# Six expert tiles run between the steps of the last batch's routing, in one block

## The reference

```python
x = x + jnp.tanh(g_xattn[0]) * _L0_xattn_ref(_layernorm(x, axis=-1), ctx_1024, L0_xattn_Wq, L0_xattn_Wkv, L0_xattn_Wc)
x = x + jnp.tanh(g_ffn[0]) * _L0_ffn_ref(_layernorm(x, axis=-1), L0_ffn_gate_w, L0_ffn_w1, ...)
# in _L0_ffn_ref:
logits = jnp.einsum('btd,de->bte', x, gate_w)
top_v, top_i = jax.lax.top_k(logits, TOP_K)
top_w = jax.nn.softmax(top_v, axis=-1)
comb = jnp.zeros((N, E), dtype=x.dtype).at[jnp.arange(N)[:, None], idx].add(wts)
for e in range(E):
    h = jax.nn.gelu(xf @ w1[e] + b1[e], approximate=False)
    out = out + comb[:, e:e + 1] * (h @ w2[e] + b2[e])
```

## Time and profile before

| what | value |
|---|---|
| device time, median of 3 runs | 993.09 us (992.86 to 994.03) |
| span of the profiled execution | 992.7 us |
| PE busy | 832.3 us, 84% of the span |
| DVE, POOL, ACT busy | 517.9, 438.1, 376.7 us |
| share of PE in the chain that ended last | 43%; issue 1%, DMA 1%, all else under 1% |

### The profile page before, as it was taken

One profiled execution on the slowest core, in us unless ns is written; L12 is line 12 of the kernel. 1 busy time (PEld: TensorE's weight loads), 2 busy tenths in 40 slices (PEclk: granted clock), 3 DMA queues, 4 the chain that ended last, 5 costly groups with the idle time before them and its releaser, 6 DMA issues. The chain is left out here.

```text
span 992.7 us, 20863 instructions
## 1 busy us (share of the span) xinstructions
PE 832.3 (84%) x6508; PEld 579.8 (58%) x6509; DVE 517.9 (52%) x1534; ACT 376.7 (38%) x770; POOL 438.1 (44%) x475
## 2 busy tenths in 40 slices
PE   3675899899898989887610899999999999999994
PEld 1243345344343534433310699899989989988984
DVE  3475567766766677762330345444544454454451
ACT  1312263636363544666320333333333433333330
POOL 4766463666566545436541033333433343333334
PEclk9867899989997989898755799999999999999998
DMA  4653424433445261244224122221332233223210
GB/s 160 147 108 107 75 66 90 129 82 108 97 128 98 64 136 49 82 134 138 77 74 165 56 44 46 48 45 33 56 48 41 43 58 48 43 47 49 44 14 1
DMA packets 65691, 76.40 MB, mean 77 GB/s; under 512 B 7392, under 2 KB 59360, under 8 KB 65504
## 3 DMA queue, kind: packets, MB, share of 16 engines
q1 hardware_dynamic: 51328, 58.74, 22.7%
q0 software_dynamic: 14304, 16.93, 9.6%
HBM read 47.68 MB, written 29.53 MB: 78 GB/s over the span
## 5 line engine op out<-in xcount | busy, mean ns | idle before, releaser
L2389 PE MATMUL ps_h<-x_hi,w_split 128*128 128x256 bf16 x1248 | 212.7, 274 | 0.0
L2403 PE MATMUL ps_y<-w_split,hidden 128*128 x1248 | 206.4, 273 | 0.0
L698 ACT ACTIVATE prob<-ps_a 128x512 f32<-128x512 f32 x192 | 113.0, 603 | 181.5 <-PE ps_a L1127 108.2
L2389 PE MATMUL ps_h<-x_lo,w_split 128*128 128x256 bf16 x624 | 171.0, 274 | 0.0
L2403 PE MATMUL ps_y<-w_split,h_lo 128*128 x624 | 170.1, 273 | 0.0
L2299 ACT ACTIVATE hidden<-ps_h,bias 128x256 f32<-128x256 f32 x312 | 131.1, 471 | 88.6 <-PE ps_h L2389 88.6
L849 DVE TENSOR_REDUCE row_max<-ps_d 128x2 f32<-128x384 f32 x237 | 127.9, 551 | 60.8 <-PE ps_d L1107 59.2
L2273 POOL DMA_INDIRECT out<-y,token_at x78 | 131.0, 1680 | 43.8 <-POOL token_at L2271 30.3
L2389 PEld LDWEIGHTS ps_h<-x_hi,w_split 128*128 x1248 | 122.8, 98 | 14.5
L2403 PEld LDWEIGHTS ps_y<-w_split,hidden 128*128 128x128 bf16 x1248 | 122.1, 98 | 14.1
L2269 POOL TENSOR_TENSOR token_f<-tails,ones_f 128x2 f32<-128x2 f32 x39 | 7.8, 200 | 267.5 <-DVE y L2345 266.3
(11 more groups left out here) (206 smaller groups left out, 1070.8 us busy)
## 6 DMA issues: line engine op xcount, KB each, us to landing
w_stage<-w SPq DMA_DIRECT2D x32, 512.0 KB, 4.1
xg<-queue SPq DMA_DIRECT2D x39, 260.0 KB, 2.8
w_split<-q_split SPq DMA_DIRECT2D x24, 256.0 KB, 7.9
x_in<-x SPq DMA_DIRECT2D x8, 512.0 KB, 3.8
ctx_sb<-ctx_t SPq DMA_DIRECT2D x8, 512.0 KB, 3.6
x<-x SPq DMA_DIRECT2D x8, 512.0 KB, 3.8
q_split<-q_hl SPq DMA_DIRECT2D x16, 256.0 KB, 3.5
out<-x SPq DMA_DIRECT2D x8, 512.0 KB, 5.0
```

Of the source, the lines that this page charges most:

```text
L698: a.activation(prob[n % 2][:, j, :], ps_a[i % 2][:], ACT.Exp, scale=SCALE).then_inc(exp_ready, 1)
L2389: last = t_.matmul(ps_h[n][:, c, :], k.w1_split[:, bass.ds(e, 1), part, kt, f].rearrange("p a f -> p (a f)"), xs[s][:, kt, :], start=(q == ...
L2403: last = t_.matmul(ps_y[s][:, t, :], hs[s][:, f, token], k.w2_split[:, bass.ds(e, 1), part, f, :].rearrange("p a d -> p (a d)"), start=(q ...
```

## The change

The passes stop after p = 7. The last batch's routing now shares a new stretch with the first six tiles (`EARLY`). These are full tiles of 256 rows, taken from what the first six batches have put into the queues; `early_tables` on DVE works them out in pass 7, at step 2. The stretch is a list of 44 parts, `tile_parts()`: quarters of `layer1` and `layer2` (12 matmuls each), and the routing steps, now numbered by part (`END_*`), stand between them. `layer2` of tile 5 is left to the loop. The queues' remaining rows make 33 more tiles (`late_tables`). There is one block: no end of block stands between the two halves, and `in_general` comes between the stretch of 44 parts and the loop. PSUM is shared: `ps_x` is the bank `ps_r`, `ps_h` the banks `ps_d` and `ps_a`, and `ps_y` is the one bank `ps_o`, where before there were two. In the parts each quarter reads the expert number for itself. The last four pieces of the weights, the scatters of batches 6 and 7 and the adds of tiles 0 to 4 fall into the same stretch.

```diff
+EARLY = 6
+EARLY_BATCHES = 6
+PAIRS = FC // 2
...
+def early_tables(v, chain, k, scratch, ready, count):
+
+    chain.then(v.tensor_scalar(k.pad_f[:], k.n_queued[:], -float(TILE - 1), None, ALU.add))
+    tile_tables(v, chain, k, scratch, 0, EARLY, k.pad_f, k.queue_at)
+    chain.step(v.tensor_scalar(k.tiles_end[:], k.tiles_end[:], float(EARLY), None, ALU.min))
+    chain.then(v.tensor_scalar(k.tiles_start[:], k.tiles_start[:], float(EARLY), None, ALU.min))
+    chain.then(v.tensor_tensor(k.taken[:], k.tiles_end[:], k.tiles_start[:], ALU.subtract))
+    chain.then(v.tensor_scalar(k.taken[:], k.taken[:], float(TILE), None, ALU.mult))
+    v.tensor_tensor(k.rest_at[:], k.queue_at[:], k.taken[:], ALU.add).then_inc(ready, 1)
+    chain.engine.wait_ge(ready, count)
...
+        SP_EARLY, DVE_EARLY, PE_EARLY, ACT_EARLY = 18, 2, 29, 31
+        END_PIECES = (0, 12, 15, 18)
+        END_WEIGHTED, END_SUMS, END_TURN_SUMS, END_TAKE_HEADS = 1, 2, 3, 4
+        END_TURN_HEADS, END_COPY_HEADS, END_OUT, END_ADD, END_STATS = 5, 6, (7, 8), (8, 9), (9, 9, 10, 10)
+        END_MOMENTS, END_DEVIATION, END_SHIFT, END_ROWS = 10, 11, 12, 13
+        END_TURN_ROWS, END_COPY_ROWS, END_GATE, END_COPY_GATE, END_TURN_GATE = 15, 16, 17, 18, 19
+        END_CHOOSE, END_RATIO, END_RANK, END_SHARES, END_QUEUE = 20, 21, 22, 22, 23
...
+        def tile_parts():
+
+            parts = []
+            for i in range(EARLY):
+                parts += [(1, i, n) for n in range(PAIRS)]
+                if i:
+                    parts += [(2, i - 1, n) for n in range(PAIRS)]
+            return parts
...
         def each_step():
-            for p in range(-4, B + 2):
+            for p in range(-4, B):
...
+            chain.restart()
+            for step, (layer, i, n) in enumerate(tile_parts()):
+                if step == 0:
+                    queue_slots(LAST - 1)
+                    k.prepare(dve, chain, 0)
+                if step == END_TAKE_HEADS:
+                    take_heads(LAST, QUAD - 1)
...
+                if step == END_QUEUE:
+                    queue_slots(LAST)
+                    pad_places(v, chain, k, pads_placed)
+                    dve.wait_ge(pads_placed, 1)
+                    late_tables(v, chain, k, heads[:].rearrange("p t d -> p (t d)"), k.tables_ready, 3)
+                if layer == 1:
+                    if n == 0 and i + 1 < EARLY:
+                        k.prepare(dve, chain, i + 1)
+                    k.low(dve, i, n)
+                elif n == PAIRS - 1:
+                    k.finish(dve, i)
...
+            for step, (layer, i, n) in enumerate(tile_parts()):
+                if step == END_WEIGHTED:
+                    weighted(LAST, UNITS - 1)
+                if step == END_TURN_SUMS:
+                    turn_sums(LAST, QUAD - 1)
...
+                if layer == 1:
+                    if n == 0 and i + 1 < EARLY:
+                        turn_tile(i + 1)
...
+                    k.layer1(pe, i, n)
+                else:
+                    if (i, n) == (0, 0):
+                        bank_o.wait_read(pe)
+                    k.layer2(pe, i, n)
+            pe.wait_ge(w_lo, N_PIECES)
...
+        def layer1(pe, i, n, at=None, e=None):
+            s, _ = slot_of(i, at)
+            e = load_expert(pe, i) if e is None else e
...
+            turn(pe, EARLY)
+            all_layer2(pe, EARLY - 1)
             over_tiles(pe, body)
-            layer2(N_TILES - 1, (N_TILES - 1) % 2)
+            all_layer2(pe, N_TILES - 1)
```

More of the change, by code:

```diff
@@ L18 @@
 FAR = 1e30
+Q_AT = (5, 7, 6)
 SLOT_TILES = 2
@@ new lines, in split_x, with gelu @@
+        def split_x(act, i, at=None):
+            s, _ = slot_of(i, at)
+            act.wait_ge(x_turned, i + 1)
+            nc.scalar.copy(x_hi[s][:], ps_x).then_inc(x_hi_ready, 1)
+        def gelu(act, i, n, at=None):
+            s, _ = slot_of(i, at)
+            if n == 0 and not first(i, 2):
+                act.wait_ge(y_summed, i - 1)
+            act.wait_ge(h_ready, PAIRS * i + n + 1)
+            for c in range(2):
+                f = 2 * n + c
+                last = nc.scalar.activation(hidden[s][:, f, :], ps_h[n][:, c, :], ACT.Gelu, bias=bias[s][:, f:f + 1])
+            last.then_inc(gelu_done, 1)
@@ new lines, in experts, with all_layer1, all_layer2 @@
+        k.load, k.load_bias, k.add, k.split_x, k.gelu = load, load_bias, add, split_x, gelu
+        k.prepare, k.low, k.finish, k.turn, k.layer1, k.layer2 = prepare, low, finish, turn, layer1, layer2
+        def all_layer1(pe, i, at=None):
+            e = load_expert(pe, i)
+            for n in range(PAIRS):
+                layer1(pe, i, n, at, e)
+        def all_layer2(pe, i, at=None):
+            e = load_expert(pe, i)
+            for n in range(PAIRS):
+                layer2(pe, i, n, at, e)
@@ L2302, in _ @@
-            split_x(0, 0)
+                    gelu(act, i, n, (s, half))
+            split_x(act, EARLY)
             over_tiles(act, body)
@@ new lines, in early @@
+                late_tables(v, chain, k, scratch, k.tables_ready, 5)
+                for i in range(EARLY):
+                    prepare(dve, chain, i)
+                    for n in range(PAIRS):
+                        low(dve, i, n)
+                    if i:
+                        finish(dve, i - 1, early=added_again)
+                after_add(dve, EARLY - 2, added_again)
+                chain.restart()
+            pipeline.dve(dve)
+            in_general(dve, general[0].dve, general[1].dve, nothing, early)
@@ L2408, in body @@
+            pipeline.pe(pe)
+            in_general(pe, general[0].pe, general[1].pe, nothing, early)
             def body(i, half, s, more, two_more):
                 if more:
-                    turn(i + 1, half + s, 1 - s)
-                layer1(i, s)
-                if not first(i):
-                    layer2(i - 1, 1 - s)
-            turn(0, 0, 0)
+                    turn(pe, i + 1, (1 - s, half + s))
+                all_layer1(pe, i, (s, half))
+                if after_early(i):
+                    all_layer2(pe, i - 1, (1 - s, None))
```

607 lines of the change are left out of this document (391 added, 216 removed).

## The result

The changed kernel takes 964.51 us (median of 4 runs, 963.72 to 966.45); before it was 992.98 (4 runs, 991.54 to 994.03). The ratio is 0.9714, with a 95% interval of 0.9694 to 0.9734. The profiled execution has a span of 964.3 us. One execution among the experiments, of branch_else, took 1233.77 us at a mean granted clock of 0.647, where the kernel's other six had 0.938 to 0.945; the ratios leave it out.

The account below looks back on a forecast made before the run. PE bounds the loop at 10.92 us a tile but idles in the routing stretch before it. Loop start 581.6, plus 365.6 for tiles, 2.0 low clock and 13.1 end, gave span 962.3, median 963; own range 957 to 969, wider 946 to 977.

Parts of the forecast that it names:

- lateness by the early tables: Pass 7: `early_tables` ahead of `take_heads` on DVE delays batch 6's routing; 2.3 us remain, bounds 0 and 3.8.
- waits on the routing: In the 44 parts PE waits for routing pieces from other engines: 6.4 us, of which 2.4 at the turn of tile 2.
- register reads: In the 44 parts each quarter's read of the expert number outlasts PE's lead: 13 us, bounds 0 and 19.
- low clock: At the start of the stretch PE, nearly idle before, runs at half speed: 2.3 us.
- gap at the branch: `in_general` between quarter 44 and the loop leaves PE idle for 4.2 us, bounds 2.5 and 4.55.
- low clock behind it: A second low-clock spell after PE's idle gap at the branch: 2.0 us, bounds 0 and 4.
- rival of hidden loads: In the stretch PE's sequencer runs ahead, so some 3 of the 13 us of loads remain: 951 us, chance 0.25.
- rival of more waits: PE's waits let the clock fall inside the stretch, and lateness grows to 3.8: 970 to 980 us, chance 0.13.
- rival of half clock in all of the stretch: The stretch stays at half clock, about 141 us in place of 90.7: 1013 us, chance 0.03.
- One bank for `ps_y`: Rival: layer2 waits for the previous tile's `finish`; 4.2 us of loop room, else up to 1011 us; chance 0.05.
- The hidden chain: Scatter, pads and load of first loop rows end about 83 us into the stretch, ahead of PE at 95.
- 0.4 between span and median: Last step of the sum: the median stands 0.4 us above the profiled span, so 962.3 gives 963.

Follow-up runs that it names:

- branch_else: The changed kernel with the loop written on both sides of the branch, so the branch is not taken with these inputs: 959.35 us, ratio to before 0.9671.
- one_load: The changed kernel with PE reading the expert number once for four quarters, 11 reads in place of 44: 951.21 us, ratio to before 0.9588.
- no_general: The changed kernel without the read of `wide`, its branch and the general program: 959.63 us, ratio to before 0.9664.
- three_else: The changed kernel with one register read per four quarters, weight piece at part 6, `take_heads` one part earlier, loop on both branch sides: 943.56 us, ratio 0.9518.
- early4: The changed kernel with four early tiles in place of six (`EARLY = 4`): 973.52 us, ratio to before 0.9803.

## Why the prediction was right

The forecast was 963 with a range of 946 to 977; 964.51 lies in it. The steps, against the profiled execution, where each measured term is a difference of rows of its trace:

| step | predicted us | measured us |
|---|---|---|
| opening, up to the end of `slot_f` of batch 5 | 447.16 | 444.27 |
| lateness by the early tables | 2.3 | 3.3 (0.2 where pass 7 is without the spell) |
| `prepare` of tile 0 | 1.8 | 2.3 |
| 44 parts | 90.7 | 92.84 |
| of these, waits on the routing | 6.4 | 7.0 |
| of these, register reads | 13 | 10.9 undone in one_load, some 12.8 with the waits that grew |
| of these, low clock | 2.3 | 3.4 |
| gap at the branch | 4.2 | 3.66 |
| low clock behind it | 2.0 | 3.2 (1.6 in one_load) |
| 33 tiles, less the first turn | 359.9 | 361.7 |
| end | 13.1 | 11.9 |

**Register reads.** This term decided between the forecast and its first rival, and it held: the loads cost, and 0.40 a quarter was 0.43 in the text. What the rival of hidden loads describes had to be written first: one_load takes 951.21, where the rival had 951. That the two agree so closely is partly luck, since the branch's gap, 2.5 in the rival, is still 3.7 in one_load. That a lead of PE's sequencer hides two reads a tile in the loop stays argued; shown is that a read for every 12 matmuls is not hidden. The Trainium skill (Advanced Engine Details and Errata, Sequencer Loop) has other instructions read and queued while one executes; no run here shows how far.

**Waits.** The size was right, the cause of the largest only half. The step said that gelu, `low` and `take_heads` in a row make 2.4 us ahead of the turn of tile 2. 2.79 were measured, but with a `low` of 3.0 us in it, behind POOL's weight piece, which the step had left out. Without the piece it is 2.28, the sum of the step. Not named at all was a wait of 1.1 us for `h_lo`, at `layer2` of tile 3: the tables for the late tiles stand on DVE ahead of the `low`, `finish` and `prepare` that PE needs next.

**Clock.** The low clock at the start and behind the branch was there, and a third spell came behind the wait for `heads`, as the rival of more waits had it; the stretch cut in three:

```profile
485.29:493.00 7.71, 7.46 (x49) 4.82 (x49) 2.59 (x9) 5.03 (x9) 6.04 (x6) 0.77 0.77 210
493.00:502.80 9.80, 6.59 (x40) 5.06 (x41) 6.07 (x12) 3.02 (x7) 3.10 (x2) 0.83 0.58 187
502.80:578.13 75.33, 63.95 (x525) 48.44 (x523) 35.38 (x119) 26.99 (x56) 31.91 (x31) 1.00 0.36 83
```

7.71 x 0.23 and 9.80 x 0.17 make 3.4 us. The rest ran at 1.00. The rival of half clock in all of the stretch, of which there is no sign, had a slip in its sum: twice 69.0 and the waits of 6.4 are 144, not 141.

**Branch.** The row was right for PE's branch, 3336 ns after 3750. The figure of 108 ns in the Trainium skill (Advanced Engine Details and Errata, Control Flow Timing) is near the branch that is not taken, 93 ns. The rest fits another page of the Trainium skill, Runtime: NRT & Kernel Launch, section Instruction fetch mechanics, by which a taken branch breaks the sequential prefetch; no row here shows the fetch itself. The low clock behind the gap cost 3.2 here and 1.6 in one_load, either side of the 2.0 of the sum.

**One bank for `ps_y`.** In the loop the room of 4.2 us holds, and there is no wait from 590.67 to 930, where PE is busy throughout. The rival bites where two `layer2` follow each other with no `layer1` between, which the prediction did not look for. That is so twice in this kernel. At `layer2` of tile 5 the gap of the branch hides it; without the gap PE waits 1.3 us there in no_general and 1.39 in three_else. At the last tile it shows:

```profile
PE ps_o L2520 <- DVE y L2476: 1.7, 1, 1.7
```

Part of this comes back, since POOL, which before waited for the previous add to land, now waits for DVE alone. Before and after:

```profile
982.45 0.18 POOL L2269 TENSOR_TENSOR token_f<-tails,ones_f 128x2 f32<-128x2 f32 x1 [1.22 <-DMA out<-y,token_at]
```

```profile
954.66 0.18 POOL L2416 TENSOR_TENSOR token_f<-tails,ones_f 128x2 f32<-128x2 f32 x1 [2.50 <-DVE y L2479]
```

From the end of the last matmul to POOL's start it was 2.9 us before and is 2.3 now. That is half of what makes the end 11.9 and not 13.1; the other 0.6 lie behind POOL's start and stay open.

**The hidden chain.** The rows of the first loop tile were issued at 565.61 and take 2.9 us, so they were there 83 us behind the start, as worked out; PE came 96.5 behind it. early4 shows the price without this cover.

**From span to median.** The step that was wrong is the 0.4 between span and median. Every execution that was listed with its span takes 1.7 to 2.3 us more than that span, so the profiled execution of before, at 992.7, was not the one of the median, and none of the four times of before in the result lies that far above it. For the change, 964.3 goes with 966.45, the longest of its four; the median goes with a span of some 962.4, where the sum gave 962.3. That agreement is partly luck. In the profiled execution the opening ended 2.9 us earlier than the sum took it, and most of the other errors in the table go the other way: all told its span is 2.0 longer than the sum.

## What to carry to other kernels

Work cut into small pieces pays its fixed costs per piece: look at what the sequencer does for each piece against how long the engine takes for it, and keep registers across pieces. A wait that stands at one place can have two causes side by side, and undoing one shows nothing; undo both before you drop either. Where a path is nearly always the same, let it be the one that does not jump, and see whether a gap also costs the clock behind it.

## What was not expected of the hardware

A DVE instruction with two inputs in SBUF took 3.0 us in place of 0.69 beside one POOL instruction of 2.14 us, and 0.69 again with that moved; it ended 0.55 us behind POOL's. A branch costs PE 93 ns when not taken, and 3336 to 3750 when it leads over the general program. One and the same program had a spell of low clock of some 3 us in pass 7 in some of its profiled executions and not in others, and the opening, up to `slot_f` of batch 5, ended between 443.6 and 447.4 us.
